# Attention scores on 64 stacked rows: high and low keys of four heads side by side, low keys moved by DMA

## What is computed

```python
q = split_heads(layernorm(x) @ Wq + bq)          # (32, 16, 56, 8)
k = split_heads(ctx @ Wk + bk)                   # (32, 16, 1500, 8)
v = split_heads(ctx @ Wv + bv)
scores = einsum('bhqd,bhkd->bhqk', q, k) / sqrt(8)
scores = where(mask == 0, -1e9, scores)
x = x + (softmax(scores) @ v) @ Wo + bo
x = x + bitlinear(gelu(bitlinear(layernorm(x), w1)), w2)
```

## Time and profile before

| | |
|---|---|
| Median of three runs | 959.67 us |
| The profiled execution | 959.75 us |
| Its span, first to last instruction | 958.0 us |
| Granted TensorE clock, mean over the span | 0.976 of full speed |
| PE, DVE, ACT, POOL busy | 887.8, 753.1, 673.4, 231.5 us |
| Read from HBM | 47.91 MB |

### The profile page before, as it was taken

The page is one execution under the profiler, slowest core; times in us unless marked ns, Lnnn a source line. Parts: engine busy times, 40 slices in busy tenths (PEclk is TensorE's granted clock), DMA queues, the critical chain, the costliest instruction groups (busy, mean ns, idle before and its releaser), DMA issues.

```text
span 958.0 us, 33628 instructions
## 1 busy us (share of the span) xinstructions
PE 887.8 (93%) x11716; PEld 694.2 (72%) x11716; DVE 753.1 (79%) x2593; ACT 673.4 (70%) x1272; POOL 231.5 (24%) x253
## 2 busy tenths in 40 slices
PE   3767989999999999999999999999999999999983
PEld 2344767777787787778787777777787777778772
DVE  3687568888788878888788888888787888888744
ACT  2543667777887877777886777777887777777661
POOL 6310142230222222130222222131222222031200
PEclk9788999999999999999999999999999999999997
DMA  5520221122222211122222211122222111220000
GB/s 130 127 62 1 63 61 29 42 57 60 63 60 63 59 34 47 46 60 60 63 60 63 53 32 50 51 60 60 63 60 61 49 32 50 56 60 0 4 2 6
DMA packets 59375, 49.34 MB, mean 52 GB/s; under 512 B 2785, under 2 KB 55633, under 8 KB 59345
## 3 DMA queue, kind: packets, MB, share of 16 engines
q1 hardware_dynamic: 57551, 48.11, 19.0%
q10 hardware_dynamic: 1793, 0.83, 0.4%
HBM read 47.91 MB, written 0.92 MB: 51 GB/s over the span
## 4 chain that ended last, share of the span: by engine, by line
issue 66%; POOL 18%; PE 7%; DVE 5%; ACT 1%; DMA 1%; POOLq 1%; DVEq 0%; ACTq 0%
POOL k_lo L573 8%; POOL qry_hi L565 4%; POOL qry_lo L566 4%; PE ps_p L820 2%; DMA ctx_sb<-in_ctx_dram 1%; PE ps_p L803 1%; DVE max_junk L1091 1%; POOL q_lo L563 1%; POOL q_hi L562 1%; PE ps_v L856 1%; PE ps_p L744 1%; ACT probs L659 1%; POOL x_rows L581 0%; PE ps_p L741 0%; POOLq L556 0%
## 5 line engine op out<-in xcount | busy, mean ns | idle before, releaser
L1091 DVE CUSTOM_DVE_ANT_0 max_junk<-ps_p,mask_bias 120x500 bf16<-120x500 f32 x768 | 481.6, 675 | 125.3 <-PE ps_p L803 104.5
L659 ACT ACTIVATE probs<-ps_p 125x448 f32<-125x448 f32 x768 | 359.3, 551 | 87.0 <-PE ps_p L820 81.6
L573 POOL TENSOR_TENSOR k_lo<-k_full,k_hi 128x500 fp32r<-128x500 f32 x96 | 119.8, 1262 | 592.0 <-ACT k_hi L651 587.2
L856 PE MATMUL ps_v<-probs,vals 125*32 125x112 f32 x6144 | 162.9, 262 | 0.8 <-issue 0.4
L803 PE MATMUL ps_p<-k_hi,qry_hi 64*120 64x500 f32 x768 | 148.8, 413 | 15.6 <-POOL qry_hi L565 6.5
L820 PE MATMUL ps_p<-qry_hi,k_hi 64*125 64x448 f32 x768 | 158.6, 403 | 4.4 <-DVE seg_max L1091 1.7
L856 PEld LDWEIGHTS ps_v<-probs,vals 125*32 125x32 f32 x6144 | 146.9, 111 | 21.1 <-issue 17.7
L641 ACT ACTIVATE k_full<-ps_p,bk_sb 128x500 f32<-128x500 f32 x96 | 64.7, 674 | 123.1 <-PE ps_p L744 122.6
L820 PE MATMUL ps_p<-own_query,mask_bias 57*125 57x448 f32 x768 | 145.7, 368 | 0.0
L820 PE MATMUL ps_p<-qry_lo,k_hi 64*125 64x448 f32 x768 | 144.4, 366 | 0.0
L820 PE MATMUL ps_p<-qry_hi,k_lo 64*125 64x448 f32 x768 | 144.3, 365 | 0.0
(11 more groups left out here) (124 smaller groups left out, 831.5 us busy)
## 6 DMA issues: line engine op xcount, KB each, us to landing
ctx_sb<-in_ctx_dram SPq DMA_DIRECT2D x31, 750.0 KB
mask_sb<-in_mask_Bx1xSxS_ik_dram SPq DMA_DIRECT2D x64, 328.1 KB
own_query<-shift SPq DMA_DIRECT2D x64, 1.8 KB
out_dram<-x_rows SPq DMA_DIRECT2D x16, 56.0 KB, 1.6
ctx_sb<-in_ctx_dram ACTq DMA_DIRECT2D x1, 750.0 KB
x_rows<-in_x_dram SPq DMA_DIRECT2D x1, 672.0 KB, 10.9
w_sb<-in_L_ffn_w_dram SPq DMA_DIRECT2D x2, 256.0 KB, 8.8
x_rows<-in_x_dram SPq DMA_DIRECT2D x1, 224.0 KB, 5.9
```

The costliest lines, as they stand in the source:

```text
L573: pool.tensor_tensor(k_lo[:, p, at], k_full[:, (p + n) % 2, :], k_hi[:, p, at].bitcast(F32), ALU.subtract)\
L659: act.activation(probs[:, c % NP, h], ps_p[0:KC, BANK[how]["S", c, h], 0:HC], ACT.Exp)\
L856: mm = pe.matmul(ps_v[r:r + VT, col:col + PAIR], vals[:, p, c, t].rearrange("p a r -> p (a r)"), src, start=(c == 0 and t < 4), stop=(c == ...
L1091: dve.tensor_tensor_reduce(max_junk[0:MROWS, BANK[how][slot], :], ps_p[0:MROWS, BANK[how][slot], 0:SEG], mask_bias[0:MROWS, p, s * SEG:(s ...
```

## The change

- Keys: `k_hi` and `k_lo` [128 rows, 2, 1500] give way to `keys` [128 rows, 2, 2 groups, 1500]. Of the 64 rows of a half, 32 belong to each group of four heads. In group 0 the first 32 rows hold high keys of those four heads and the other 32 rows their low keys; in group 1 it is the other way round. ScalarE's kh writes 1000 columns in place of 500 (the high keys, once for each group). GpSimd writes the low keys of a segment to a small buffer, and SP copies them by four DMAs of 32 rows and 500 columns each (`place_low`) over the rows of `keys` that are not the group's own. TensorE waits for these copies (`k_lo_placed`), and GpSimd waits for older ones before it writes the small buffer again.
- Queries: the projection is made twice, with the columns of Wq (and bq) in two orders, so that both 32-row parts hold the query of the same head (`wq_sb`, `q_all`, Q0 to Q7 for Q0 to Q3; N_WQ 2 to 12 DMAs). `q_flag`, `q_hi`, `q_lo` have 112 columns for 56. `qry_lo` is zero on the rows of low keys (`head_of_high`).
- Scores: for each group, one pair of matmuls with `qry_hi` (high and low keys at once) and one with `qry_lo`, 224 columns each; then mask and shift with 448 columns. So five pairs in a chunk: four of 224 columns and one of 448, in place of four of 448.
- Maxima (M) read `keys`, with the same sizes.
- SP's steps: `place_low` calls stand among load, store and `place_shift`, also in the start.
- `probs` has eight buffers for twelve. All orders of TensorE, ScalarE and VectorE are written anew, and GpSimd's odd order.

The core of the diff:

```diff
-NP = NC
+NP = 2 * NG
 PE_EVEN = order("""
-    T0 T1 V0 M0 s0 f0 M1 S1 S2 M2 S3 M3 S4 S5 M4 S6 S7 M5 M6 P0 D0 K0 M7 S8 S9 M8 S10 M9 O0 S11 M10 M11 T2 K1 F0
-    V1 V2 K2 R0 P1 P2
+    T0 T1 D0 V0 M0 s0 M1 f0 S1 S2 M2 S3 M3 S4 M4 S5 M5 O0 K0 M6 M7 M8 P0 S6 M9 S7 S8 M10 S9 S10 M11 S11 F0 K1 T2
+    V1 R0 V2 K2 P1 P2
 """)
 ACT_EVEN = order("""
-    T0 T1 V0 e0 e1 e2 e3 e4 e5 e6 e7 e8 e9 e10 e11 e12 e13 e14 e15 sum0 kf0 e16 e17 e18 e19 e20 e21 e22 kh0 e23
-    T2 kf1 kh1 kf2 V1 V2 kh2
+    T0 T1 V0 e0 e1 e2 e3 e4 e5 e6 e7 e8 e9 e10 e11 sum0 kf0 kh0 e12 e13 e14 e15 e16 e17 e18 e19 e20 e21 e22 T2
+    e23 kf1 V1 kf2 kh1 V2 kh2
 """)
 PE_ODD = order("""
-    V0 T0 H0 s0 M0 f0 S1 S2 M1 S3 S4 M2 M3 G0 P0 M4 S5 M5 S6 S7 M6 S8 S9 M7 S10 S11 M8 M9 P1 P2 M10 M11 K0 U0 V1
-    T1 Y0 T2 D0 K1 F0 K2 R0 V2
+    M0 s0 f0 S1 M1 S2 S3 M2 T0 H0 V0 G0 M3 M4 S4 P0 M5 S5 S6 S7 S8 M6 D0 V1 T1 K0 F0 M7 S9 S10 S11 M8 U0 K1 T2
+    Y0 M9 M10 M11 P1 P2 K2 R0 V2
 """)
 ACT_ODD = order("""
-    sum0 V0 T0 e0 e1 e2 e3 e4 e5 e6 e7 e8 e9 G0 e10 e11 e12 e13 e14 e15 e16 e17 e18 e19 e20 e21 e22 e23 kf0 kh0
-    T1 V1 T2 kf1 kh1 kf2 V2 kh2
+    sum0 e0 e1 e2 e3 e4 e5 e6 e7 T0 V0 G0 e8 e9 e10 e11 e12 e13 e14 e15 e16 e17 T1 V1 kf0 e18 e19 e20 e21 e22
+    e23 kf1 T2 kh0 kh1 kf2 V2 kh2
 """)
 DVE_ODD = order("""
-    H0 own0 m0 m1 m2 m3 m4 m5 m6 m7 m8 m9 m10 m11 hid0 m12 m13 bias0 m14 m15 hid1 m16 some0 hid2 hid3 m17 bias1
-    m18 m19 m20 m21 U0 m22 m23 neg0 Y0 bias2 D0 R0 F0
+    m0 m1 m2 m3 bias0 some0 m4 H0 m5 own0 m6 m7 m8 m9 m10 m11 hid0 hid1 hid2 m12 m13 D0 m14 F0 m15 hid3 U0 m16
+    m17 Y0 bias1 m18 bias2 m19 m20 m21 m22 m23 neg0 R0
 """)
...
+            def place_low(bt, n):
+                b, k, p = bt
+                made = NSEG * b + n + 1
+                at = slice(n * SEG, (n + 1) * SEG)
+                sp.wait_ge(k_lo_ready, made if isinstance(b, int) else sp.snap(made))
+                for h in range(2):
+                    for g in range(2):
+                        src, dst = SLOT * h + GR * g, SLOT * h + GR * (1 - g)
+                        sp.dma_start(keys[dst:dst + GR, p, g, at].bitcast(F32), k_lo[src:src + GR, (p + n) % 2, :].bitcast(F32))\
+                            .then_inc(k_lo_placed[p][n], 16)
...
             def step(bt):
                 b, k, p = bt
                 loop = not isinstance(b, int)
-                if loop or b + 3 < B:
-                    load(later(bt, 3))
-                if p == 1 and (loop or b > 1):
-                    store(bt)
-                if loop or b + 1 < B:
-                    place_shift(later(bt, 1))
+                if p == 0:
+                    if loop or b + 3 < B:
+                        load(later(bt, 3))
+                    if loop or b + 2 < B:
+                        place_low(later(bt, 2), 0)
+                    if loop or b + 1 < B:
+                        place_shift(later(bt, 1))
+                    if loop or b + 2 < B:
+                        place_low(later(bt, 2), 1)
+                    if loop or b + 2 < B:
+                        place_low(later(bt, 2), 2)
+                else:
+                    if loop or b + 3 < B:
+                        load(later(bt, 3))
+                    if loop or b > 1:
+                        store(bt)
+                    if loop or b + 2 < B:
+                        place_low(later(bt, 2), 0)
+                    if loop or b + 2 < B:
+                        place_low(later(bt, 2), 1)
+                    if loop or b + 1 < B:
+                        place_shift(later(bt, 1))
+                    if loop or b + 2 < B:
+                        place_low(later(bt, 2), 2)
...
+            for n in range(NSEG):
+                place_low(batch(0, 0), n)
             sp.dma_start(wo_sb[:], wo).then_inc(wo_loaded, 16)
...
+            for n in range(NSEG):
+                place_low(batch(0, 1), n)
             place_shift(batch(0, 0))
...
-                act.activation(k_hi[:, p, at], k_full[:, (p + n) % 2, :], ACT.Copy).then_inc(k_hi_ready, 1)
+                act.activation(keys[:, p, :, at],
+                               k_full[:, (p + n) % 2, :].rearrange("p (g k) -> p g k", g=1).to_broadcast([D, 2, SEG]),
+                               ACT.Copy).then_inc(k_hi_ready, 1)
...
-                    pe.wait_ge(k_hi_ready, NSEG * b + s + 1)
+                    pe.wait_ge(k_lo_placed[p][s], 64 * (k + 1))
...
+            def products(bt, c, how):
+                b, k, p = bt
+                at = slice(c * KC, (c + 1) * KC)
+                for g in range(2):
+                    heads = slice(GH * g, GH * (g + 1))
+                    for part, query in enumerate((qry_hi[:, p, heads, 0:SQ], qry_lo[:, p, heads, :])):
+                        for h in range(2):
+                            rows = slice(SLOT * h, SLOT * (h + 1))
+                            pe.matmul(score_bank(c, h, how)[:, heads, :], keys[rows, p, g, at], query[rows],
+                                      start=(g == 0 and part == 0), stop=False,
+                                      skip_group_check=True)
```

More of the change, by code:

```diff
@@ L142 @@
     "T0 T1 T2 sum kf0 kh0 kf1 kh1 kf2 kh2 V0 V1 V2",
[L143 removed]
+    ACT_EVEN, ACT_ODD, "G0", {"e11": "abs", "e5": "X1", "kf0": "X2"}, {"e9": "X3"})
 DVE_PASS = passes(
[L145 removed]
+    "Q0 Q1 some F0 bias0 bias1 bias2",
     " ".join(f"m{n}" for n in range(16)) + " some " + " ".join(f"m{n}" for n in range(16, 21))
@@ L307, in xattn_ffn @@
         k_lo_ready = sem("k_lo_ready")
+        k_lo_placed = [[sem(f"k_lo_placed{p}_{n}") for n in range(NSEG)] for p in range(2)]
         vals_ready = sem("vals_ready")
@@ L658, in exp @@
                     act.wait_ge(scores_ready, NC * b + c + 1)
-                act.activation(probs[:, c % NP, h], ps_p[0:KC, BANK[how]["S", c, h], 0:HC], ACT.Exp)\
+                act.activation(probs[:, (c + NG * p) % NP, h], ps_p[0:KC, BANK[how]["S", c, h], 0:HC], ACT.Exp)\
                     .then_inc(exp_done, 1)
@@ L757, in fill @@
                 elif kind == "Q":
-                    mm = pe.matmul(bank[:, 0:4 * PAIR], wq_sb[:], xnt[:, n % 2, :], start=True, stop=True)
+                    mm = pe.matmul(bank[:, 0:4 * PAIR], wq_sb[:, n % 2], xnt[:, n // 2 % 2, :], start=True, stop=True)
                 elif kind == "Z":
@@ L804, in maxima, with score_bank, shifts @@
                               qry_hi[rows, p, 2 * r:2 * r + 2, :].rearrange("p a q -> p (a q)")[:, 0:MROWS],
-                              k_hi[rows, p, s * SEG:(s + 1) * SEG], start=True, stop=True)\
+                              keys[rows, p, r // 2, s * SEG:(s + 1) * SEG], start=True, stop=True)\
                         .then_inc(bank_full[BANK[how]["M", n, h]], 1)
-            def score(bt, c, how, first, last):
+            def score_bank(c, h, how):
+                return ps_p[0:KC, BANK[how]["S", c, h], 0:HC].rearrange("k (a q) -> k a q", a=HH)
+            def products(bt, c, how):
                 b, k, p = bt
                 at = slice(c * KC, (c + 1) * KC)
-                hi, lo, bias = k_hi[:, p, at], k_lo[:, p, at], mask_bias[:, p, at]
-                q_hi_of, q_lo_of = qry_hi[:, p, :, 0:SQ], qry_lo[:, p, :, :]
-                products = [(hi, q_hi_of, HR), (lo, q_hi_of, HR), (hi, q_lo_of, HR),
-                            (bias, own_query[:, p, :, :], SQ + 1)]
-                for n in range(first, last):
-                    key, query, rows = products[n]
-                    for h in range(2):
-                        part = slice(SLOT * h, SLOT * h + rows)
-                        mm = pe.matmul(ps_p[0:KC, BANK[how]["S", c, h], 0:HC].rearrange("k (a q) -> k a q", a=HH),
-                                       key[part, :], query[part], start=(n == 0), stop=(n == 3))
+                for g in range(2):
+                    heads = slice(GH * g, GH * (g + 1))
+                    for part, query in enumerate((qry_hi[:, p, heads, 0:SQ], qry_lo[:, p, heads, :])):
+                        for h in range(2):
+                            rows = slice(SLOT * h, SLOT * (h + 1))
+                            pe.matmul(score_bank(c, h, how)[:, heads, :], keys[rows, p, g, at], query[rows],
+                                      start=(g == 0 and part == 0), stop=False,
+                                      skip_group_check=True)
+            def shifts(bt, c, how):
+                b, k, p = bt
+                for h in range(2):
+                    rows = slice(SLOT * h, SLOT * h + SQ + 1)
+                    mm = pe.matmul(score_bank(c, h, how), mask_bias[rows, p, c * KC:(c + 1) * KC],
+                                   own_query[rows, p, :, :], start=False, stop=True, skip_group_check=True)
                 return mm
```

98 lines of the change are left out of this document (61 added, 37 removed).

## The result

The changed kernel takes 969.88 us (median of four runs, 968.91 to 974.28) where the kernel before takes 959.49 us beside it (958.06 to 964.99): a ratio of 1.0111, interval 1.0067 to 1.0156. It is about 1% slower; 930 us was forecast. The profiled execution took 970.35 us, its span is 968.6 us.

A forecast was written before the change was run, and what follows sets the result against it. TensorE's work was taken to bound the kernel. A round: -4.1 + 0.25 + 1.0 + 0.5 = -2.35 us; 16 rounds -37.6, start +8, so 959.75 - 29.6 = 930 us; range 898 to 998, 8 in 10.

The forecast's parts named there:

- the scores' pace: TensorE's score matmuls: pairs of 224 columns take 0.109 us, a chunk 0.64, saving 4.1 us a round.
- Rival A: TensorE's scores: short pairs stay at 0.2025 us whatever their columns, +4.9 us a round, 1049 us; chance 0.13.
- tiling: TensorE's changes of tile size: 0.13 us each, 18 in a round instead of 16, +0.25 us a round.
- kh: ScalarE's writing of high keys, 1000 columns for 500: from 0.619 to 1.05 us, hidden beside TensorE's work.
- neighbours: TensorE waiting more often for banks that VectorE and ScalarE haven't yet taken: +1.0 us a round, at most 3.
- Rival C: Neighbouring engines set the pace: TensorE's waits for banks cost 3.0 us a round instead of 1.0, 962 us; chance 0.15.
- an exponential wait for P: Sign of a wrong forecast: ScalarE's exponentials wait for P with `probs` at eight buffers; taken as 0.
- SP's issues: SP's queue: 0.45 us per low-key copy, eight in 3.6; shift 1.1 us late, room 1.1, +0.5 us a round.
- rival B: SP's queue: each copy's issue takes 1.0 us, shift 5.5 us late, a wait of 4.4 a round, 993 us; chance 0.12.
- turning point: SP's queue: the rival of slow copy issues decides from a wait of 2.35 us a round, 0.74 us an issue.
- the start: Work before the rounds: first shift at 53.95 us instead of 49.24, Wq's second order +3; +8 us in all (0 to 15).
- PE idle over 3 us a round: Sign on TensorE listed beforehand as showing the forecast wrong: idle for more than 3 us in each round.

The follow-up runs named there:

- e9: Changed kernel with the shift issued before segment 1's copies in odd steps and 279 satisfied waits at the start of TensorE's program: 927.14 us, ratio 0.9668.
- e10: Changed kernel as it is, with 279 satisfied waits at the very start of TensorE's program: 945.74 us, ratio 0.9859.
- e4: Changed kernel with the shift issued before the copies of segment 1 in odd steps, no added waits: 967.32 us, ratio 1.0075.
- e3: Kernel before the change with 345 satisfied waits ahead of TensorE's loop, which move it by 172 instructions: 1077.85 us, ratio 1.1198.
- e8: Changed kernel with all engines' orders as in the kernel before and 278 satisfied waits ahead of TensorE's loop: 1088.57 us, ratio 1.1329.

## Why the prediction was wrong, step by step

**Right: the scores' pace.** 0.11 us a pair and 0.64 a chunk, as forecast. Rival A is out, and these rows speak against the Trainium skill's rule on row groups too (TensorE: Matmul & The Clock Gate, Part 3, The mechanism): a pair with a new load of 125 columns for the same 64 rows follows every 0.11 us. (The same section also lets a load into the background weight buffer go ahead of running matmuls; the trace doesn't say which buffer a load takes.)

**Right in sum, not in parts: tiling, kh, neighbours.** kh takes 1037 ns (forecast 1050, gave the basis):

```profile
L713 ACT ACTIVATE keys<-k_full 128x1000 fp32r<-128x1000 f32 x96 | 97.8, 1037 | 0.6
```

The forecast's round without any wait for the shift was 54.17 - 4.1 + 0.25 + 1.0 = 51.3 us; e9, which has none, has 51.34. That the sum came out is in part luck. Take the time from each matmul's start to the next one's and add it up by line, over twelve rounds each: from the kernel before to e9 the scores fall by 3.5 us a round (20.65 to 17.16) and not by 4.1, the maxima rise by 1.7 (6.62 to 8.31), where all changes of tiling and all waits were to cost 1.25, and the rest falls by 1.0, the contexts' transposes alone by 0.6 (3.20 to 2.62), for which the forecast had no term. Rival C is out. Nor did an exponential wait for P.

**Mis-sized: SP's issues.** The prediction took 0.45 us per copy, from eight small loads. The timeline of SP's queue in e10, a round without code loading:

```profile
405.04 4.97 SPq L456 DMA_DIRECT2D keys<-k_lo  x8
410.06 1.44 SPq L444 DMA_DIRECT2D own_query<-shift  x2
```

4.97 us for eight, 0.62 each (0.59 in a copy's own record, the median); the forecast had 3.6, and the shift 1.1 us late with 1.1 of room. These issues alone are 1.4 us longer. In e10's timeline of PE the pair of chunk 0 that needs the shift stands idle before its start:

```profile
411.18 0.43 PE L868 MATMUL ps_p<-keys,qry_hi 64*120 64x500 f32 x2
412.64 0.47 PE L894 MATMUL ps_p<-own_query,mask_bias 57*125 57x448 f32 x2 [1.04 <-DMA own_query<-shift]
```

Against e9 the shift's position costs 52.63 - 51.34 = 1.29 us a round, where 0.5 was taken, and 18.6 us in all. This is rival B's mechanism, below its turning point: by the forecast's own working 0.62 gives a wait of about 1.4. In the changed kernel the same eight take longer still:

```profile
406.97 6.55 SPq L456 DMA_DIRECT2D keys<-k_lo  x8
413.57 1.44 SPq L444 DMA_DIRECT2D own_query<-shift  x2
```

Six of them take 0.52 to 0.59 us as in e10, and two take 1.09 and 1.67. This is the code loading once more (last section).

**Off in its parts: the start.** The first shift leaves SP at 60.17 us and not at 53.95:

```profile
52.33 7.80 SPq L456 DMA_DIRECT2D keys<-k_lo  x12
60.17 1.47 SPq L444 DMA_DIRECT2D own_query<-shift  x2
```

Twelve copies take 7.8 us, not 5.4. The loop's first branch, two rounds into the work, comes 5.2 us later than before (191.2 against 186.0), where the forecast's +8 less two rounds' 2.35 would be +3.3, and the time behind the last branch is 3.5 us shorter (64.4 against 67.9).

**The step that failed: none of the sum was it, it was missing.** The prediction counted what the engines do and wait for, and took the code itself as free. Its own list had named the sign, "PE idle over 3 us a round", and no rival had that cause. The changed kernel's round is 54.85 us; e10's, the same work with the loop in seven blocks, 52.63: **2.22 us a round**, 29 over 13 rounds, less what e10's waits cost at the start; between the medians 969.88 - 945.74 = 24 us. The stall itself is larger, 3.1 to 3.4 us in 12 of 13 rounds from the last matmul's start before it to the first one's behind it (38.9 us together). It cost less than its length because it covers the shift's wait of 1.29 us: two delays at one place in the round, of which only the longer is paid. The changed kernel's own quick round shows it, 52.61 us and the one wait for the shift in it. Thus e4's fix alone was worth 2.6 us at most, and both together 43.

The clock took the rest. In three of the rounds the granted clock fell behind the stall, and these last 55.9 to 57.2 us, the other nine with a stall 54.3 to 54.9. The windows view after, columns as in the earlier trace rows, at one of the three:

```profile
634.00:682.00 48.00, 47.58 (x752) 36.18 (x749) 42.96 (x151) 40.25 (x74) 13.14 (x13) 1.00 0.33 86
682.00:688.00 6.00, 3.06 (x19) 2.87 (x19) 0.94 (x3) 2.91 (x5) 1.24 (x1) 0.75 0.30 71
688.00:694.00 6.00, 6.00 (x51) 5.15 (x52) 3.67 (x10) 2.81 (x7) 0.00 (x0) 0.68 0.32 86
```

PE was full up to 682, then stood for half of the next 6 us; a value between 0.5 and 1 is a stretch with both of the clock's levels.

**The account,** by medians: before to e9, the change with its scores and orders and without its two delays, -32 us (959.35 to 927.14), of which the idle waits take back some 5; the shift behind the copies, +19 (to e10's 945.74); code loading, +24 (to 969.88). The forecast of 930 us lies 3 us from e9 and 40 from the kernel that was timed.

## What to carry to other kernels

Before pricing a change that adds instructions to a loop, count the engine's instructions in it and see where it begins and ends in blocks of 256: on PE seven blocks were free here and an eighth cost a branch of 3.4 to 5.1 us in nearly every round. The profile shows it as "issue" idle time at the loop's first work and as packets of 16384 bytes on the instruction queue. And a fix measured alone may show nothing while another delay at the same place covers it: the shift's order was worth 2.6 us in e4, within the scatter, and 18.6 between e10 and e9.

## What the runs showed that was not expected

- The same work with its loop at another place in the code can take 12% longer: e3, 1077.85 against 959.85 us, for a loop moved by 172 instructions; some 22 of the 118 us were lost ahead of the first branch.
- Idle waits aren't free: 139 of them cost 12 us ahead of the loop (first branch 203.0 against 191.2 us) and 5 to 9 us at the very start (196.0 against 191.2, and 194.6 against 186.0). How these arise no run shows.
- Loading PE's code also holds up SP. A copy of low keys, 32 rows of 2000 bytes within SBUF, takes SP 0.59 us in e10, e8 and the changed kernel alike (median of the records). But of the changed kernel's copies from 190 us on 46 take 0.66 to 1.91 us, and every one of the 46 overlaps in time with a packet of the instruction queue (so do 43 that aren't long); in e10 none of these copies is long. How a packet stretches an issue no run shows.
